# Window attention and router: fp32 products of 32x32 tiles in place of fp16 parts, with a new order of work on five engines

## What is computed

```python
def xattn(x, cond):                       # 8 heads of 32 channels, window of 16
    q, k, v = pointwise(Wq, x), pointwise(Wk, cond), pointwise(Wv, cond)   # with biases
    k_win, v_win = window(k), window(v)   # 8 to the left, 7 to the right, zero padded
    attn = softmax(einsum('bhdt,bhdtw->bhtw', q, k_win) * 32 ** -0.5)
    return pointwise(Wo, einsum('bhtw,bhdtw->bhdt', attn, v_win))
def ffn(h):                               # 64 experts, top 8, over rows of 2048
    scores = softmax(h @ router.T + router_bias)
    w = top_8(scores)                     # kept weights, zero elsewhere
    return h * w.sum() + w @ expert_bias
x = x + tanh(g_xattn) * xattn(layernorm(x), ctx)
x = x + tanh(g_ffn) * ffn(layernorm(x))   # layernorm over the 2048 time steps
```

## Time and profile before

| | us |
|---|---|
| median of the runs (3 runs, 1550.94 to 1556.23) | 1553.8 |
| the profiled execution, its own time | 1557.26 |
| span of its trace | 1555.1 |
| PE busy | 1464.6 |
| DVE busy | 1276.5 |
| POOL busy | 1148.0 |
| ACT busy | 1144.8 |

### The profile page before, as it was taken

How to read it: one execution, slowest core, us unless ns; L and a number is a source line. 1 busy time by engine, 2 the same in 40 slices (tenths; PEclk the granted TensorE clock), 3 DMA queues, 4 the chain that set the end, 5 groups by cost and what they waited for, 6 DMA issues and landing times.

```text
span 1555.1 us, 66658 instructions
## 1 busy us (share of the span) xinstructions
PE 1464.6 (94%) x28162; PEld 1199.9 (77%) x28162; DVE 1276.5 (82%) x2970; ACT 1144.8 (74%) x2009; POOL 1148.0 (74%) x1110
## 2 busy tenths in 40 slices
PE   4799999999999999999999999999999999999985
PEld 3687887888787888878788788878888887778764
DVE  5578987888898887988888898888889888788764
ACT  4687877777787877788787877778787787767652
POOL 4688777787777877877787887778778777677661
PEclk8899999999999999999999999999999999899896
DMA  7455455445546554454555545455554545434132
GB/s 230 125 140 126 106 173 131 123 149 143 147 121 172 141 131 146 121 157 128 149 149 141 156 119 159 128 146 147 144 159 114 159 132 142 121 98 128 44 81 85
DMA packets 365577, 210.39 MB, mean 135 GB/s; under 512 B 294497, under 2 KB 295521, under 8 KB 361057
## 3 DMA queue, kind: packets, MB, share of 16 engines
q1 hardware_dynamic: 365280, 206.14, 49.1%
HBM read 136.88 MB, written 33.55 MB: 110 GB/s over the span
## 4 chain that ended last, share of the span: by engine, by line
PE 46%; DVE 35%; issue 8%; POOL 5%; ACT 3%; DMA 2%; SPq 1%; POOLq 0%; DVEq 0%; ACTq 0%
PE ps_j L1117 18%; PE ps_s L1177 7%; PE ps_a L1142 6%; PE ps_r L1219 5%; DVE prob_t L900 5%; PE ps_s L1117 3%; DVE p_sum L890 3%; DVE st_x L907 2%; DVE wq_lo L822 2%; POOL prob L493 2%; DVE lg L1046 2%; DVE st_in L804 2%; DVE v_turn L871 2%; PE ps_s L1172 2%; PE ps_a L1196 2%
## 5 line engine op out<-in xcount | busy, mean ns | idle before, releaser
L486 POOL TENSOR_TENSOR score<-score,p_inv 128x384 f32<-128x384 f32 x256 | 221.6, 866 | 119.5 <-DVE p_inv L894 117.0
L493 POOL TENSOR_TENSOR prob<-score,prob 128x384 f16<-128x384 f32 x256 | 266.0, 1039 | 38.8 <-ACT prob L644 38.3
L1177 PEld LDWEIGHTS ps_s<-kv_win,q_col 32*32 32x32 f32 x16384 | 198.0, 107 | 57.8 <-issue 57.8
L1177 PE MATMUL ps_s<-kv_win,q_col 32*32 32x48 f32 x16384 | 234.1, 205 | 2.4 <-issue 2.2
L900 DVE STREAM_TRANSPOSE prob_t<-prob 128x512 f32<-128x512 f32 x256 | 176.7, 699 | 55.1 <-POOL prob L493 54.9
L467 POOL TENSOR_TENSOR c_lo<-c_in,c_hi 128x1024 fp32r<-128x1024 f32 x64 | 152.7, 2386 | 89.5 <-ACT c_hi L618 89.5
L1142 PEld LDWEIGHTS ps_a<-prob_t,v_diag 128*128 128x128 f16 x6528 | 175.3, 98 | 50.1 <-DVE prob_t L900 32.6
L1142 PE MATMUL ps_a<-prob_t,v_diag 128*128 128x48 f16 (+2 forms) x6528 | 187.6, 183 | 26.2 <-DVE prob_t L900 19.4
L462 POOL TENSOR_TENSOR att_lo<-att,att_hi 128x512 fp32r<-128x512 f32 x128 | 161.8, 1275 | 51.5 <-ACT att_hi L604 50.3
L1117 PE MATMUL ps_j<-c_hi,wkv_hi 128*128 128x512 f32 x512 | 171.3, 416 | 19.6 <-DVE kv_win L864 10.6
L890 DVE TENSOR_REDUCE p_sum<-score 128x8 f32<-128x384 f32 x256 | 139.2, 544 | 54.3 <-ACT score L638 53.6
(11 more groups left out here) (149 smaller groups left out, 3318.0 us busy)
## 6 DMA issues: line engine op xcount, KB each, us to landing
v_diag<-v_turn SPq DMA_DIRECT2D x512, 68.0 KB, 2.8
c_in<-ctx_dram SPq DMA_DIRECT2D x64, 512.0 KB, 4.9
x_in<-x_dram SPq DMA_DIRECT2D x64, 512.0 KB, 5.5
x_res<-x_dram SPq DMA_DIRECT2D x64, 512.0 KB, 4.3
out_dram<-x SPq DMA_DIRECT2D x32, 1024.0 KB, 7.0
c_sq<-ctx_dram SPq DMA_DIRECT2D x60, 512.0 KB, 5.5
x<-ctx_dram SPq DMA_DIRECT2D x4, 512.0 KB, 6.1
x<-experts_dram SPq DMA_DIRECT2D x2, 512.0 KB, 10.6
```

The source lines that it names most:

```text
L486: pool.tensor_tensor(score[:, u], score[:, u], p_inv[:, u, :].unsqueeze(2).to_broadcast([P, HALF, KEYS]), ALU.mult).then_inc(pm_rdy, 1)
L493: pool.tensor_tensor(part(prob[:, u % 2], 1)[:, :, 0:KEYS], score[:, u], part(prob[:, u % 2], 0)[:, :, 0:KEYS], ALU.subtract).then_inc(pl_ ...
L1177: ins = pe.matmul(s[head(h), n * KEYS:(n + 1) * KEYS], q_col[head(h), g, at:at + SUB], kv_win[c % 2][head(h), 0, g, at:at + KEYS], start=F ...
```

## The change

The scores and the attention output are both small fp32 products of 32x32 tiles now; the fp16 halves and everything that fed them are gone.

- **Attention output**: `attend(g, late, off)` issues 4 products per block of keys, one per head, of a 32x32 tile of `v_turn` with 48 columns of `prob_t`: 68 products (136 records) per group, in an early part of 8 blocks and a late part of 9. `v_diag`, its DMAs, `low`, `high`, `values_low`, the sum of squares and the second load of the context are gone.
- **Mask**: DVE adds it when it takes the scores out of PSUM (`masked`); the mask product is gone. `largest` reads that copy in SBUF, and `shift` is POOL's.
- **Router**: rows and weights are split into fp32r parts (`turn_hi`, `turn_lo` by ACT and DVE; `wr_both` holds both parts of the weights side by side). Eight fp32r products of 256 columns a step; once per sequence ACT copies the sums (`logit_sums`), and PE adds the two halves (`fold_logits`, two products). Router weights and logits stay in PSUM (`wd`, `lg`).
- **Query weights**: ACT writes `wq_ln` and `wq_hi`, POOL `wq_lo` (DVE before).
- **Order**: keys of a chunk are projected before its values, the values one step later. Group 1 comes before group 0 in several places. Stores go out in quarters of 256 KB, in the step after. The first loads are ordered anew.

```diff
@@ sync: first loads and stores
+            sp.dma_start(wkv_raw[:, 1], wvT.rearrange("(g p) o -> p g o", g=G)).then_inc(wv_ld, 16)
+            sp.dma_start(c_in[:], ctx[0, :, cols(0)].rearrange("(g p) t -> p g t", g=G)).then_inc(ctx_in, 16)
+            sp.dma_start(wkv_raw[:, 0], wkT.rearrange("(g p) o -> p g o", g=G)).then_inc(wk_ld, 16)
...
-            for ch in range(NCH):
-                sp.dma_start(x1[0][:, :, cols(ch)],
-                             ctx[0, :, cols(ch)].rearrange("(g p) t -> p g t", g=G)).then_inc(sq0_ld[ch], 16)
...
-                        for h in range(HPG):
-                            sp.dma_start(v_diag[head(h), g, :, head(h)],
-                                         v_turn[head(h), g].rearrange("p (j d) -> p j d", d=SUB)).then_inc(vd_ld[g], 16)
...
-                    sp.dma_start(rows_out, x1[1 - par][:, g, :]).then_inc(out_st[g], 16)
+                    sp.dma_start(out[done, g * P:(g + 1) * P, cols(j)], x1[done % 2][:, g, cols(j)]).then_inc(out_st[g], 16)
@@ gpsimd
-                    pool.tensor_tensor(part(prob[:, u % 2], 1)[:, :, 0:KEYS], score[:, u],
-                                       part(prob[:, u % 2], 0)[:, :, 0:KEYS], ALU.subtract).then_inc(pl_rdy, 1)
+                    need(pool, mx_rdy[u], nth(b, c, off))
+                    pool.tensor_tensor(rows, rows, neg_max[:, u, :].unsqueeze(2).to_broadcast([P, HALF, KEYS]),
+                                       ALU.add).then_inc(sh_rdy[u], 1)
@@ vector
-                    dve.tensor_tensor(score[:, u], scores_of(u), neg_max[:, u, :].unsqueeze(2).to_broadcast([P, HALF, KEYS]),
-                                      ALU.add).then_inc(sh_rdy, 1)
+                    need(dve, s_mm[u], nth(b, c, off))
+                    need(dve, pt_rdy[u], nth(b, c, off - 1))
+                    dve.tensor_tensor(score[:, u, :, 0:KEYS], ps_s[u % 2][:, 0:HALF * KEYS].rearrange("p (n k) -> p n k", k=KEYS),
+                                      mask[:].unsqueeze(1).to_broadcast([P, HALF, KEYS]), ALU.add).then_inc(mk_rdy[u], 1)
...
+                    need(dve, xth_rdy[g], nth(b, c, off))
+                    dve.tensor_tensor(turn_lo[:, :, g], ps_t[:].rearrange("p (k t) -> p k t", k=TB), turn_hi[:, :, g],
+                                      ALU.subtract).then_inc(xtl_rdy[g], 1)
...
-                        dve.scalar_tensor_tensor(lg[:, g, 0], wd[:, g, 0:E], rs_x1[:, g:g + 1], rb[:],
+                            dve.scalar_tensor_tensor(lg[:, g], wd[:, g], rs_x1[:, g:g + 1], rb[:],
                                                  ALU.mult, ALU.add).then_inc(small, 1)
@@ tensor
-                def attend(g):
+                def attend(g, late, off):
 
-                    need(pe, pt_rdy, done(UNITS, b, c, -1, 2 * g + 1))
-                    need(pe, vd_ld[g], nth(b, c, -1) * (16 * HPG))
-                    need(pe, ae_rdy[g], nth(b, c, -2))
+                    need(pe, pt_rdy[2 * g + late], nth(b, c, off))
+                    if not late:
+                        need(pe, vt_rdy[g], nth(b, c, off))
+                        need(pe, ae_rdy[g], nth(b, c, off - 1))
...
-                    for j in range(BLKS):
+                    for j in range(HALF, BLKS) if late else range(HALF):
...
-                        for n, (kv, kp) in enumerate(((0, 0), (1, 0), (0, 1))):
-                            ins = pe.matmul(ps_a[g][:, q0:q1], part(v_diag[:, g, j], kv),
-                                            part(prob_t[:, g, lo:hi], kp),
-                                            start=(j == 0 and n == 0), stop=(j == NB), skip_group_check=True)
+                        for h in range(HPG):
+                            ins = pe.matmul(ps_a[g][head(h), q0:q1], v_turn[(c + off) % 2][head(h), g, j * SUB:(j + 1) * SUB],
+                                            prob_t[head(h), g, lo:hi],
+                                            start=(j == 0), stop=(j == NB), skip_group_check=True)
...
-                    pe.matmul(s[:, 0:HALF * KEYS], ident_b[:], mask[:].rearrange("p n k -> p (n k)"),
-                              start=True, stop=False, skip_group_check=True)
...
-                            ins = pe.matmul(ps_r[:, g * E:(g + 1) * E], x1_t[:, g, k], wr[:, ch * TB + k],
-                                            start=(ch == 0 and k == 0 and g == 0),
-                                            stop=(ch == NCH - 1 and k == TB - 1), skip_group_check=True)
+                        for n, v in enumerate((turn_hi, turn_lo)):
+                            ins = pe.matmul(ps_r[:, ACC], wr_both[:, ch * TB + k], v[:, k].rearrange("p g c -> p (g c)"),
+                                            start=(ch == 0 and k == 0 and n == 0),
+                                            stop=(ch == NCH - 1 and k == TB - 1 and n == 1))
```

1180 lines of the change are left out of this document (551 added, 629 removed).

## The result

| | median of the runs | against before | profiled execution |
|---|---|---|---|
| before | 1555.0 us (1550.9 to 1557.5) | 1 | 1555.1 us of span |
| after | 1613.8 us (1612.6 to 1620.6) | 1.038, 95% interval 1.0355 to 1.0404 | 1612.0 us of span |

The changed kernel is slower by 3.8%, where 1505 us and a range of 1468 to 1550 had been predicted. The views answer to those of before as follows. First the page: its row for PE, the row of the queue that brings in instructions, and the last chain.

A forecast was written before the change was run, and what follows sets the result against it. PE's list was taken to bound the kernel unless a loop through the other engines became longer. Steps -31, start -16 and end -2 us from 1555.1 made 1506 of span, about 1505 us measured; range 1468 to 1550.

The forecast's parts named there:

- PE's list: PE's work per step, summed from the durations of its groups: a change of -0.25 us, hardly anything.
- +0.90: Attention output on PE: two groups of 136 records at 12.8 ns each, 3.48 us against 2.58 a step.
- The eight router products: Router on PE: eight fp32r products of 256 columns take 1.0 us in place of 1.81, -0.8 a step.
- The bounds on the list: Limits on the change of PE's work per step: -1.1 and +1.4 us, or +3.1 with 25 ns records.
- the loop through POOL: From `rows(1)` through ACT and POOL back to PE: 21.1 us, setting the pace in steps without mixtures.
- Rival 3: POOL ends slower, idling 6 us a step: a step of 23.6 us, 1586 us in all; chance 0.12.
- a sign of being wrong: POOL's idle time above 5.5 us a step in the trace after would show the forecast wrong.
- the 0.6 us for the layer-norm chain: Step of c = 3: DVE's chain now stands ahead of `masked(0)`, adding 0.6 us, for 23.6 in all.
- contention with POOL for one line: DVE's logits at L1046: with the first input in PSUM, DVE gains 1.3 us in a c = 1 step.
- Rival 2: Tiles take turns in the bank, 272 records at 25 ns: +3.3 us a step, 1713 us; chance 0.03.
- Start: First projection at 10 us, first scores near 33: a gain of 16 us, at least 8, at most 20.
- The end: Last store becomes 256 KB, the fold adds a copy and two products: -2 us, bounds -4 and +1.

The follow-up runs named there:

- e4: The changed kernel with `attend` for heads 0 and 1 of each group only, half of the attention output left out: 1508.2 us, 0.972 against before.
- e5: The kernel before with 36 small fp32 products of 32x32 tiles added ahead of the mask in scores(1) and scores(2), 288 instructions a step: 1787.9 us, 1.151.

## Why the prediction was wrong

**The step that failed is the pricing of PE's list by durations alone.** It said "Two groups of 136 records make 3.48 against 2.58: +0.90", and the row that it took, one unit of scores at 12.8 ns a record, was right or a little dear: the groups of the changed kernel take 0.79, 0.77 and 1.52 us. The eight router products take 1.14 from the first to what follows them, where 1.0 had been put. But that row stood alone between longer products. The list had no term for the instructions themselves. 10,112 more records in 64 steps are 158 a step, 316 instructions with their weight loads, and three or four groups of small products now stand close together. Pauses are 1.7 us a step, 1.5 more than before, and the step came out 1.6 above its forecast (23.9 against 22.3). None of the rivals was this mechanism. It was readable: 28,162 records in 223 packets, stops of "issue" in the attention and score lines, 5.3 and 2.2 us, where small products already stood in a row. They were in the views, and I passed over them as small. (The bounds on the list were also added wrongly: by its own terms they are -1.0 and +0.9, or +4.2 with 25 ns a record, in place of -1.1, +1.4 and +3.1. Nothing hangs on it.)

**Less the pauses, the forecast of the step is nearly right.** The four kinds of step take 20.6, 21.7, 22.8 and 25.0, mean 22.5, where 21.1, 21.4, 23.0 and 23.6 had been forecast, mean 22.3. That the means agree this well is partly luck: errors of -0.5, +0.3, -0.2 and +1.4 offset one another.
- c = 0 and 1: the loop through POOL was forecast to bind and doesn't. The step of c = 0 without pauses is 0.5 us shorter than it, and in the whole trace PE waits for the residual in 3 places (2.5 us in all) and for `att_lo` in one (1.0).
- Rival 3 (POOL idles, slower) has the sign of the result but not its cause. The prediction had named POOL's idle time above 5.5 us a step as a sign of being wrong, and it is 7.0 by the windows view, (1400 - 991) / 1400 of 23.9 us. But POOL is idle because what it waits for comes later: e4 leaves POOL's list as it is, takes instructions off PE alone, and the time falls by 106 us.
- c = 3: the 0.6 us for the layer-norm chain ahead of `masked(0)` was mis-sized. Its new place beside `c_lo` makes it 5.8 us long, and 1.4 us more of it than forecast are on the path. The prediction had contention with POOL for one line (L1046 at 946 ns against 275), and there it came out: that instruction takes 283 ns now (L840). I didn't ask which instructions the new order would bring beside POOL's long ones.
- Rival 2, the tiles taking turns in the bank at 25 ns a record, is out: 11 to 13 ns.

**Start.** The first projection came at 10.71 (10 forecast), but the second chunk's keys waited for POOL (29.24), and the first scores came at 41.14, not 33:

```profile
29.24 1.22 PE L1003 MATMUL ps_j<-c_hi,wkv_hi 128*128 128x512 f32 x2 [11.08 <-POOL c_lo L446]
...
41.14 0.88 PE L1061 MATMUL ps_s<-kv_win,q_col 32*32 32x48 f32 x64
```

The gain is 11.3 us at the first router, inside the bounds of 8 and 20, below the 16. The end lost 1 us where 2 were to be gained; that was not followed up.

**The sum.** 1555.1 - 11.3 + 67 + 1 = 1612. Against the forecast's 1506: 98 us in the steps, of which the pauses that before didn't have are about 95, then 5 us at the start and 3 at the end.

## What to carry to other kernels

Price a list of small instructions twice: by their durations, and by their number against the rate at which instructions come in. Here the packets of some 256 PE instructions started 3.2 us apart or more, so groups of small tile products that use one up in 1.6 us need long products between them. A rewrite that puts 136 records in the place of 51 has to gain more than the added instructions cost: about 5 ns of pauses for each in this change, 6 in e5, and 8 there with all that came with the pauses (139 us for 17,150). When an order changes, look at which small DVE instructions come to lie beside long ones of POOL.
